# Attention products with the values: from split fp32r matmuls to plain fp32 in two column halves of TensorE

## What is computed

```
q, k, v = split(x @ w_qkv.T + b_qkv)                    # 16 heads, 32 features each
scores  = q @ k.T / sqrt(32) + causal mask
out     = softmax(scores) @ v                           # the products that the change is about
x       = x + out @ w_out.T + b_out
```

## Time and profile before

| | us |
|---|---|
| runs | 3135.39 (median), 3135.32, 3136.49 |
| the profiled execution | 3133.39, its span 3131.6 |
| FFN 1 | 0 to 1108 |
| projection in | 1108 to 1297 |
| heads | 1297 to 1942 |
| output projection | 1942 to 2023 |
| FFN 2 | 2023 to 3132 |

### The profile page before, as it was taken

The page is one execution under the profiler, slowest core; times in us unless marked ns, Lnnn a source line. Parts: engine busy times, 40 slices in busy tenths (PEclk is TensorE's granted clock), DMA queues, the critical chain, the costliest instruction groups (busy, mean ns, idle before and its releaser), DMA issues. The chain is left out here.

```text
span 3131.6 us, 40559 instructions
## 1 busy us (share of the span) xinstructions
PE 2982.2 (95%) x13152; PEld 2307.4 (74%) x13152; DVE 1958.1 (63%) x3306; ACT 1264.6 (40%) x2213; POOL 1267.8 (40%) x880
## 2 busy tenths in 40 slices
PE   5999999999999979999999998669999999999999
PEld 3788888888888857666666664448888888888887
DVE  7656655666555564677777773576665666656664
ACT  4322222222222232488888887143222222222222
POOL 4322222222222256577777777243222222222221
PEclk8999999999999989999999999889999999999999
DMA  3000000000000028533333221300000000000001
GB/s 94 21 28 28 27 20 20 27 27 27 20 20 20 1 83 221 161 68 68 68 67 67 68 83 49 107 20 28 27 28 20 20 27 27 27 20 20 27 14 54
DMA packets 123919, 144.54 MB, mean 46 GB/s; under 512 B 71904, under 2 KB 72160, under 8 KB 120480
## 3 DMA queue, kind: packets, MB, share of 16 engines
q1 hardware_dynamic: 123256, 142.70, 16.7%
q10 hardware_dynamic: 552, 0.59, 0.1%
HBM read 105.26 MB, written 38.01 MB: 46 GB/s over the span
## 5 line engine op out<-in xcount | busy, mean ns | idle before, releaser
L60 PE MATMUL psum<-ffn_x_high,ffn_w_high 128*128 128x512 f32 x2048 | 803.6, 392 | 17.1 <-DVE ffn_gelu L388 17.0
L525 POOL TENSOR_TENSOR ffn_inner<-ffn_gelu,ffn_inner 128x512 fp32r<-128x512 f32 x256 | 346.6, 1354 | 1155.8 <-ACT ffn_inner L470 1155.8
L61 PE MATMUL psum<-ffn_x_low,ffn_w_high 128*128 128x512 f32 x2048 | 799.1, 390 | 0.0
L62 PE MATMUL psum<-ffn_x_high,ffn_w_low 128*128 128x512 f32 x2048 | 798.8, 390 | 0.0
L378 DVE SCALAR_TENSOR_TENSOR ffn_gelu<-ffn_gelu,psum 128x512 f32<-128x512 f32 x256 | 176.1, 688 | 599.0 <-ACT ffn_gelu L463 598.9
L1337 POOL TENSOR_TENSOR probs_low<-probs,probs_high 128x512 fp32r<-128x512 f32 x384 | 484.7, 1287 | 157.5 <-ACT probs_high L1298 156.2
L60 PEld LDWEIGHTS psum<-ffn_x_high,ffn_w_high 128*128 128x128 f32 x2048 | 386.2, 189 | 103.0 <-DVE ffn_gelu L388 21.0
L61 PEld LDWEIGHTS psum<-ffn_x_low,ffn_w_high 128*128 128x128 f32 x2048 | 386.2, 189 | 81.8 <-issue 2.0
L62 PEld LDWEIGHTS psum<-ffn_x_high,ffn_w_low 128*128 128x128 f32 x2048 | 385.9, 188 | 80.7
L60 PE MATMUL psum<-ffn_inner,ffn_w_high 128*128 128x512 f32 x1024 | 398.6, 389 | 0.2
L62 PE MATMUL psum<-ffn_inner,ffn_w_low 128*128 128x512 f32 x1024 | 398.4, 389 | 0.0
(11 more groups left out here) (124 smaller groups left out, 4061.8 us busy)
## 6 DMA issues: line engine op xcount, KB each, us to landing
ffn_words<-packed SPq DMA_DIRECT2D x96, 256.0 KB
ffn_word_scales<-scales SPq DMA_DIRECT2D x96, 256.0 KB
qk_parts<-parts SPq DMA_DIRECT2D x32, 512.0 KB, 4.4
queries<-qk_parts SPq DMA_DIRECT2D x48, 256.0 KB, 4.7
keys<-qk_parts SPq DMA_DIRECT2D x48, 256.0 KB, 6.8
v_parts<-parts SPq DMA_DIRECT2D x16, 512.0 KB, 6.1
values<-v_parts SPq DMA_DIRECT2D x16, 512.0 KB, 10.8
o_parts<-heads_out SPq DMA_DIRECT2D x64, 128.0 KB
```

The lines of the kernel that those rows point to most:

```text
L60: pe.matmul(out, w_high, x_high, start=first, stop=False, skip_group_check=True)
L61: pe.matmul(out, w_high, x_low, start=False, stop=False, skip_group_check=True)
L62: return pe.matmul(out, w_low, x_high, start=False, stop=last, skip_group_check=True)
L525: pool.tensor_tensor(inner[:, tb % 2, m, 1, :], product[m], f32(inner[:, tb % 2, m, 0, :]), ALU.subtract)\
```

## The change

All 40 tiles of a head are multiplied with the values in one way: plain fp32 values of 33 columns (32 and the ones), plain fp32 probabilities, one matmul (two records). Output rows 0 to 32 of a bank or 64 to 96 are written, and so the left or the right half of TensorE's columns is used, by turns. The tiles are reordered so that two "lanes" of 20 tiles alternate: blocks 3 and 0 in the left half, 2 and 1 in the right one, with equal widths in each pair. The products are not done slot by slot but four in a row after every fourth slot. Nothing of the values, probabilities or outputs is split, so L986, L1035, L1298, L1337 and L1437 go; the DRAM buffers of values and outputs halve. VectorE writes the biased values straight to the buffer that SP stores, and waits there for the store of four items before. The ring of probabilities grows from 5 to 8 tiles. A bank holds two blocks, so ScalarE evicts twice a head, 97 rows, and SP stores four DMAs for each. The chunks of maxima come in the order of blocks 3, 2, 1, 0.

```diff
-VCOLS = 2 * HD + 1
+VCOLS = HD + 1
+LANE = 64
...
+LANES = [[(b, kt) for b in lane for kt in tiles_of_block(b)] for lane in ((3, 0), (2, 1))]
+TILES = [tile for pair in zip(*LANES) for tile in pair]
+BANKS = [(3, 2), (0, 1)]
+BATCH = 4
 AHEAD = 4
-RING = AHEAD + 1
+RING = AHEAD + BATCH
...
 TensorE, product with the values
-                pe.wait_ge(probs_ready, 120 * hp + (SLOTS * s + t + 1))
+                if t % BATCH == 0:
+                    pe.wait_ge(probs_ready, 120 * hp + (SLOTS * s + t + BATCH))
                 off = max(0, kt * P - b * TB)
-                out = out_bank[b % 2][0:VCOLS, off:TB]
-                if t in WHOLE:
-                    last = pe.matmul(out, f32(values[i][:, kt, :]), probs[:, t % RING, 0:TB - off], ...)
-                else:
-                    pe.matmul(out, values[i][:, kt, :], probs_high[:, t % RING, 0:TB - off], ...)
-                    pe.wait_ge(probs_low_ready, ...)
-                    last = pe.matmul(out, values[i][:, kt, :], probs_low[:, t % RING, 0:TB - off], ...)
+                row = t % 2 * LANE
+                last = pe.matmul(out_bank[BANK_OF[b]][row:row + VCOLS, off:TB], values[i][:, kt, :],
+                                 probs[:, t % RING, 0:TB - off], ...)
...
-                    with_values(hp, s, t)
+                    if t % BATCH == BATCH - 1:
+                        for u in range(t + 1 - BATCH, t + 1):
+                            with_values(hp, s, u)
...
 ScalarE, exponentials
-                last = act.activation(probs[:, t % RING, 0:width], source, ACT.Exp, scale=SM_SCALE)
-                if t in SPLIT:
-                    last = act.activation(probs_high[:, t % RING, 0:width], source, ACT.Exp, scale=SM_SCALE)
-                last.then_inc(probs_ready, 1)
+                act.activation(probs[:, t % RING, 0:width], source, ACT.Exp, scale=SM_SCALE)\
+                   .then_inc(probs_ready, 1)
...
 GpSimd, in the heads
-                pool.tensor_tensor(probs_low[:, t % RING, 0:width], probs[:, t % RING, 0:width],
-                                   f32(probs_high[:, t % RING, 0:width]), ALU.subtract)
...
 VectorE, values in the input projection
-                    if tt >= 2:
-                        dve.wait_ge(part_low_ready, tt - 1)
-                    dve.tensor_tensor(full[:, tt % 2, :], bank[tt % ITEM_BANKS], v_bias[:], ALU.add)
+                    if tt >= ITEM_BANKS:
+                        dve.wait_ge(stored[tt % ITEM_BANKS], 16 * (tt // ITEM_BANKS))
+                    dve.tensor_tensor(f32(parts[:, tt % ITEM_BANKS, 0, :]), bank[tt % ITEM_BANKS], v_bias[:],
+                                      ALU.add)
...
 output projection
-    for part, dst in ((0, o.from_high), (1, o.from_low)):
-        queue.dma_start(dst[:, tb % 2, tiles, :], o_parts[part]...)
+    queue.dma_start(o.from_heads[:, tb % 2, tiles, :], o_heads...)
...
-                dve.tensor_tensor(from_high[:, i, k], from_high[:, i, k], from_low[:, i, k], ALU.add)
```

More of the change, by code:

```diff
@@ L571, in tiles_of_block @@
 def tiles_of_block(b):
[L573 to L579, removed]
-SLOTS = len(TILES)
-FIRST_OF_BLOCK = [t for t in range(SLOTS) if t == 0 or TILES[t - 1][0] < TILES[t][0]]
-LAST_OF_BLOCK = [t - 1 for t in FIRST_OF_BLOCK[1:]] + [SLOTS - 1]
+    diagonal = [4 * b + 3 - j for j in range(4)]
+    if b < 2:
+        return list(range(4 * b + 4))
+    spread = [kt for j in range(4) for kt in (2 * j, 2 * j + 1, diagonal[j])]
+    return spread + list(range(8, 4 * b))
+LANES = [[(b, kt) for b in lane for kt in tiles_of_block(b)] for lane in ((3, 0), (2, 1))]
+TILES = [tile for pair in zip(*LANES) for tile in pair]
+BLOCKS = (3, 2, 1, 0)
+RANK = {b: BLOCKS.index(b) for b in BLOCKS}
+CHUNKS = [(b, qt, c) for b in BLOCKS for qt in range(4 * b, 4 * b + 4) for c in range(b + 1)]
+SLOTS = len(TILES)
+FIRST_OF_BLOCK = [[tile[0] for tile in TILES].index(b) for b in BLOCKS]
+LAST_OF_BLOCK = [max(t for t in range(SLOTS) if TILES[t][0] == b) for b in BLOCKS]
+LAST_CHUNK = {b: max(m for m in range(SLOTS) if CHUNKS[m][0] == b) for b in BLOCKS}
+BANKS = [(3, 2), (0, 1)]
+BANK_OF = {b: e for e, pair in enumerate(BANKS) for b in pair}
+BANK_DONE = [max(t for t in range(SLOTS) if BANK_OF[TILES[t][0]] == e) for e in range(2)]
 SCORE_BANKS = 3
+BATCH = 4
 AHEAD = 4
-RING = AHEAD + 1
-WHOLE = [t for t in range(SLOTS) if TILES[t][1] >= 4 * TILES[t][0]]
-SPLIT = [t for t in range(SLOTS) if t not in WHOLE]
+RING = AHEAD + BATCH
 ROWS_AFTER = 4
@@ L1137, in move_sums, with attention @@
     queue.dma_start(tile if to_chip else rows, rows if to_chip else tile).then_inc(moved, 16)
-def attention(nc, bank, o_parts, sums, inverses, w_out, b_out, heads, o):
+def attention(nc, bank, o_heads, sums, inverses, w_out, b_out, heads, o):
     with ExitStack() as ctx:
@@ L1169, in _, with store @@
         def _(sp):
-            def store(h0, s, blocks=range(NTB)):
-                for b in blocks:
-                    sp.wait_ge(out_free, 4 * h0 + (4 * s + b + 1 + 2))
-                    sp.dma_start(o_parts[:, bass.ds(h0 * HD + s * HD, HD), cols(b, TB)],
-                                 heads_out[0:2 * HD, b % 2, :]).then_inc(out_stored[b % 2], 16)
-                    sp.dma_start(sums[bass.ds(h0 + s, 1), cols(b, TB)],
-                                 heads_out[2 * HD:VCOLS, b % 2, :]).then_inc(out_stored[b % 2], 16)
+            def store(h0, s, banks=range(2)):
+                for e in banks:
+                    sp.wait_ge(out_free, 2 * h0 + (2 * s + e + 1 + 2))
+                    for lane in (1, 0):
+                        b = BANKS[e][lane]
+                        row = lane * LANE
+                        sp.dma_start(o_heads[bass.ds(h0 * HD + s * HD, HD), cols(b, TB)],
+                                     heads_out[row:row + HD, e, :]).then_inc(out_stored[e], 16)
+                        sp.dma_start(sums[bass.ds(h0 + s, 1), cols(b, TB)],
+                                     heads_out[row + HD:row + VCOLS, e, :]).then_inc(out_stored[e], 16)
             heads.load(sp, 2, 2)
@@ L1366, in steps_to, with project_out @@
     return STEPS.index((tb, k)) + 1
-def project_out(nc, x, bank, o_parts, sums, inverses, o):
+def project_out(nc, x, bank, o_heads, sums, inverses, o):
     with ExitStack() as ctx:
@@ L1496, in attend @@
         o = OutProjection(nc, ctx)
-        attention(nc, bank, o_parts, sums, inverses, w_out, b_out, heads, o)
-        project_out(nc, x, bank, o_parts, sums, inverses, o)
+        attention(nc, bank, o_heads, sums, inverses, w_out, b_out, heads, o)
+        project_out(nc, x, bank, o_heads, sums, inverses, o)
 def build(nc, x_in, packed, scales, w_v, b_v, w_qk, b_qk, w_out, b_out, out):
```

163 lines of the change are left out of this document (57 added, 106 removed).

## The result

The changed kernel takes **3116.87 us** (median of four runs, 3115.5 to 3117.2) against 3135.54 us of the kernel before on the same chip: a ratio of 0.9939, with a 95% interval of 0.9922 to 0.9956. It is 18.7 us faster; 3120 was predicted. The total came out some 3 us from the forecast; its parts were much further off.

A forecast was written before the change was run, and what follows sets the result against it. TensorE, busy 95% of the span, was taken to set the pace. First 15 heads +4.5, last head -4, value projection -5 and output projection -11 gave -15.5 us, so 3120 us, range 3050 to 3185 us.

The forecast's parts named there:

- Products with the values: TensorE in each head: lanes start in program order, so products take 18.7 us, 1.1 us less than before.
- rival (a): Products in the heads: lanes overlap fully, 14.6 us a head in place of 18.7, 3054 us in all; chance 0.23.
- Modes: Entering and leaving the column mode on TensorE, ten groups a head: 2.4 us a head, bounds 0 and 4.8.
- rival (b): Mode changes in the heads cost the full 0.48 us at each of 160 groups, 3158 us in all; chance 0.18.
- I take 1.0 us back: TensorE's waits and issue, 2.6 us a head, shrink by 1.0 us; bounds 1.5 us lost, 2.6 gained.
- rival (d): A VectorE or ScalarE wait in each group costs some 2 us a head, 3150 us in all; chance 0.10.
- It just fits: Maxima in a burst: the fifth chunk, 1.9 us behind the first, needs the second taken, at about 1.8 us.
- The casts: VectorE's L747 cast in the heads, 1.08 us in the median, would come near 0.2 us with GpSimd idle.
- The last head: Last head, without maxima of a next one: 31.4 us, 4 us less than before, bounds -8 and +2.
- Value projection: VectorE's wait for GpSimd's subtraction leaves the path in the value projection: -5 us, bounds -7 and +2.
- Before the output projection: Between last head and first output product: one add (0.7 us) goes, two store issues (about 1 us) come: 0.
- Output projection: Loads of the output projection move 2 MB less and 16 adds go: -11 us, bounds -16 and -4.

The follow-up runs named there:

- run 4: Changed kernel with each group's two left-half products issued first, then the two right-half ones: 3117.02 us, 39.61 us a head.
- run 2: Changed kernel with all 40 products of a head in the left half of the columns: 3344.49 us, 54.08 us a head.
- runs 2 and 3: The pair of run 2 (3344.49 us) and the same kernel with values widened to 65 columns, so TensorE never changes its mode (3297.16 us).
- four, light maxima: Changed kernel with VectorE taking each chunk's maximum from 128 of 512 columns and exponentials scaled by 0.001: 3100.96 us, 38.37 us a head.
- run 1: Changed kernel with the six inverse loads moved ahead of the last head's stores on SP's queue: 3100.9 us, ratio 0.9891 to the kernel before.
- run 11: Changed kernel with each load of head outputs in the output projection done twice, the second into an unread tile: 3123.63 us, ratio 0.996.
- run 10: Changed kernel with the old chain of sum buffer, ScalarE copy and wait for GpSimd put back in the value projection: 3122.09 us, ratio 0.9954.
- run 8: Changed kernel with groups of eight, maxima from 128 of 512 columns and exponentials scaled by a thousandth: 3084.32 us, 37.21 us a head.

## Why the prediction was right, and where only its sum was

**Products with the values: wrong step, rival (a) in its place.** "If a product of the other lane may start only when the second half of the one before it has started" is not so (the starts in pairs, run 4). Products take 14.6 us a head and not 18.7 (run 2: a head with one lane takes 14.5 more). This term was 4.1 us a head too dear. The rows of before could not show it: in them every matmul used the whole array.

**Modes: within its bounds, 0.7 us too cheap.** 2.4 us a head were taken, half of the bound; runs 2 and 3 have 3.15. By the bound of 4.8 rival (b) would have been due; it wasn't.

**"I take 1.0 us back": wrong in sign.** What a head has over its matmuls and its changes of mode is waits and issue. The matmuls are 37.7 us before and 14.6 + 17.9 = 32.5 us in every kernel after, by the forecast's own costs; a group's changes of mode are 0.315 us:

| kernel | a head, us | modes | waits and issue | waits for maxima in the trace |
|---|---|---|---|---|
| before | 40.3 | 0 | 2.6 | 2.3 |
| forecast | 40.6 | 2.4 | 1.6 | |
| groups of two | 40.43 | 6.3 | 1.6 | none |
| groups of four (the change) | 39.55 | 3.15 | 3.9 | 3.4 |
| groups of eight | 38.97 | 1.6 | 4.9 | 4.5 |
| four, light maxima | 38.37 | 3.15 | 2.7 | 1.1 |
| eight, light maxima | 37.21 | 1.6 | 3.1 | 1.2 |

So 1.3 us a head went into waits, where 1.0 was to come back: 2.3 us too little, which is rival (d), at about its price. "It just fits" was worked out for one burst, with three banks and 0.69 us a chunk. The waits grow with the length of a group and are at the forecast's 1.6 us with groups of two, where none is for VectorE; making VectorE's chunks light takes half of the excess away in groups of four. They arise inside a burst (run 2). How the rest divides between chunks, exponentials and issue is open. VectorE's 25 of 40 us a head, held against this rival, was an average and said nothing on a burst.

The three together: -4.1 + 0.75 + 2.3 = -1.05 for the head against the forecast, and measured 39.55 - 40.6 = -1.05.

**The casts: right in length.** Maxima parts after:

```profile
L756 DVE CAST max_parts<-minus_max x64: 170/170/1201, 1255.2 to 1885.1; 128x4 fp32r<-128x4 f32 x64
```

The median fell from 1.08 us to 0.17, with GpSimd idle through the heads. The Trainium skill, "SBUF — State Buffer", section "SBUF: two separate sides", says that VectorE and GpSimd take one shared pair of ports in turn; the median agrees. What the shorter casts are worth in time no run shows.

**The last head: right sign, 1.4 us off, and two misses in it.** Its matmuls and modes are 8.0 + 0.9 + 14.6 + 3.15 = 26.7 us, 3.4 under the forecast, and it still took 32.8, so 6.1 us are waits and others where 1.4 was taken. Some 1.2 of them are TensorE's clock. The last head of run 1, and that of run 11, have the same program and took 31.56 us. These are stretches of the busy-time view, as in the earlier trace rows, the first inside the last head of the changed kernel, the second the whole last head of run 1:

```profile
1894.00:1896.00 2.00, 2.00 (x6) 0.85 (x4) 0.00 (x0) 0.41 (x1) 2.00 (x1) 0.50 0.00 0
```

```profile
1889.78:1921.34 31.56, 27.92 (x128) 10.53 (x127) 0.00 (x0) 18.95 (x39) 4.54 (x1) 1.00 0.18 62
```

In the changed kernel the granted clock was 0.50 (the level of 1.2 GHz) for 3.4 us from 1893.0 on, and halves of 512 columns started 0.78 us apart. TensorE had stood still for 2.3 us before, until 1891.65; it did so in run 1 as well, and there the clock stayed at 1.00. For the other 3.5 us the trace has waits for ScalarE's exponentials: TensorE's matmuls stand 3.0 us for them in this head, its weight loads 9.6 us. No experiment took them apart.

**Value projection: right.** The wait of the earlier trace rows went; -7.3 us up to the first exponential, just past the bound of -7, and run 10 moves that exponential back by 5.9 us; the other 1.4 us are not accounted for. The new wait for a store of four items ago isn't seen: a store of 256 KB lands in 4.6 us.

**Before the output projection: wrong, a step left out.** The 0 that was taken for "two more store issues of the last bank (about 1 us)" counted the issues and not what stands between them in SyncE's queue. The change moves the store of blocks 3 and 2 to the end of the last head, and the six loads with 6.7 us of issue behind it. It cost 11.4 us, and 15.3 of stall are to be had by moving the loads (run 1).

**Output projection: right in kind.** -8.6 us where -11 was taken and -4 to -16 was the bound; run 11 puts it on the loads.

By its own list of signs the prediction failed in one point: stages outside the heads that gain under 8 us "would make the prediction wrong", and they gained 7.3 + 8.6 - 11.4 = 4.5 us together, where 16 were forecast. The other sign, a head off by over 1.5 us, stayed out with 1.05, and that only because two errors of 4.1 and 3.05 us met.

So the forecast of 3120 us held by luck in its sum: 4.1 us a head too much for the lanes (66 us) stood against 0.75 too little for the modes (12), some 40 us too little for waits in the heads, and 11.4 us too little behind the last head.

## What to carry to other kernels

When work of a stream is gathered into groups, price the peak of each engine beside it, not its average: here VectorE's share of 60% hid bursts, and groups of four had 2.3 us a head more of waits than groups of two. Longer groups pay as long as the saved changes of mode (0.31 us a group) outweigh the longer burst; of two, four and eight, eight was best. When buffers are merged, look at when the merged one is complete and at everything that is queued behind its store; here that one order was worth nearly as much (15.3 us of stall) as the whole change gained (18.7). And check a forecast by stages even when its total is right.

## What the runs showed of the hardware that was not expected

- Two plain fp32 products with 33 weight columns in the two halves of the array's columns overlap in full: starts 5 to 13 ns apart, 0.43 us a half of a product and 512 columns, whichever is first in the program (run 4). One lane alone takes twice as long (3.62 and 1.91 us for four products).
- A change of tiling mode and back costs 0.31 us by runs 2 and 3, about 0.1 us ahead of the products and 0.2 behind them; run 8 has 0.23 us net of longer waits. The Trainium skill, "TensorEngine Tiling (Array Packing)", Key Properties, says that changing the mode drains TensorE; the runs add the price.
- A granted clock of 0.50 for 3.4 us inside the last head went with 1.2 us more (32.80 and 31.56 us). The same stall of 2.3 us stood ahead of it in run 1, where the clock did not fall.
